# A two-layer AdaLN transformer on one Trainium2 core: 25 first expert blocks instead of 22, finer weight loads, split products, fused norms and products of zeros at the start

## The reference, cut to what matters

```python
# layer 0 (mod = silu(L0_c) @ L0_wmod gives per image: shifts sa, sb, scales ca, cb, gains ga, gb)
h = _layernorm(x) * (1 + ca) + sa
x = x + ga * attention(h)            # 16 query heads, 4 key heads of 128, rms-normed q and k, causal softmax, @ Wo
h = _layernorm(x) * (1 + cb) + sb
x = x + gb * ffn0(h)                 # shared expert + 8 experts of 176, top 2 by sigmoid scores
# layer 1 (mod from L1_c, L1_wmod)
h = _layernorm(x) * (1 + ca) + sa
x = x + ga * linear_attention(h)     # q, k, v of 128; num / den with a memory M, z; @ w_o
h = _layernorm(x) * (1 + cb) + sb
x = x + gb * ffn1(h)
# ffn1(x):
t = xf * rsqrt(mean(xf * xf) + EPS) * norm_w
vals, idx = top_k(t @ gate_w.T + gate_b, 4);  G = softmax(vals) scattered to 16 experts
h = einsum('mh,eoh->emo', t, w1) + b1
a = minimum(h[..., ::2], 7);  b = clip(h[..., 1::2], -7, 7)
y = einsum('emi,edi->emd', a * sigmoid(1.702 * a) * (b + 1), w2) + b2
delta = einsum('me,emd->md', G, y);  return x + delta
```

## Time and profile before

| | us |
|---|---|
| median of 3 runs | 1037.21 (1035.75 to 1038.29) |
| profiled execution, its own time | 1028.9 |
| its span, first to last instruction | 1026.8 |
| PE busy in the span | 961.5 (94%) |
| DVE, ACT, POOL busy | 724.0, 673.0, 425.0 |
| granted TensorE clock, mean | 0.981 |

### The profile page before, as it was taken

How to read it: one execution, slowest core, us unless ns; L and a number is a source line. 1 busy time by engine, 2 the same in 40 slices (tenths; PEclk the granted TensorE clock), 3 DMA queues, 4 the chain that set the end, 5 groups by cost and what they waited for, 6 DMA issues and landing times.

```text
span 1026.8 us, 20504 instructions
## 1 busy us (share of the span) xinstructions
PE 961.5 (94%) x6020; PEld 816.3 (79%) x6020; DVE 724.0 (71%) x2545; ACT 673.0 (66%) x1944; POOL 425.0 (41%) x447
## 2 busy tenths in 40 slices
PE   6999999999999999999999999997889989999970
PEld 4769878888987887887888788886668879999970
DVE  3565656777776777778679677874888868888870
ACT  2656767668668757858776876783745557777740
POOL 2322421332371362156137215414155655566672
PEclk9999999999999999999999999998999999999995
DMA  9926993895699620011012004226357898899944
GB/s 306 305 91 205 377 377 112 307 377 185 235 366 374 230 85 2 4 73 63 1 53 85 1 2 167 74 114 260 84 165 170 227 251 228 214 225 225 225 107 82
DMA packets 93677, 180.53 MB, mean 176 GB/s; under 512 B 9901, under 2 KB 29037, under 8 KB 92669
## 3 DMA queue, kind: packets, MB, share of 16 engines
q1 hardware_dynamic: 73467, 148.55, 43.6%
q0 software_dynamic: 18752, 30.30, 13.1%
q10 hardware_dynamic: 1346, 0.36, 0.2%
HBM read 77.71 MB, written 107.99 MB: 181 GB/s over the span
## 4 chain that ended last, share of the span: by engine, by line
PE 83%; DVE 7%; issue 3%; DMA 2%; ACT 1%; POOL 1%; ACTq 0%; DVEq 0%; SPq 0%; POOLq 0%
PE bank L1101 12%; PE bank L1065 10%; PE bank L1037 10%; PE bank L1110 5%; PE bank L1055 5%; PE bank L1027 5%; PE bank L1016 4%; PE bank L987 3%; PE bank L893 3%; PE bank L1056 3%; PE bank L902 3%; PE bank L1046 2%; PE bank L1026 2%; PE bank L971 2%; PE bank L1009 2%
## 5 line engine op out<-in xcount | busy, mean ns | idle before, releaser
L1896 POOL TENSOR_TENSOR RB<-RB 128x512 f32<-128x512 f32 x64 | 66.7, 1042 | 276.1 <-DVE RB L1675 275.9
L1101 PE MATMUL bank<-RB 128*128 128x128 f32 x1264 | 154.9, 276 | 5.2 <-ACT RB L1373 2.3
L1101 PEld LDWEIGHTS bank<-RB 128*128 128x128 f32 x1264 | 147.9, 192 | 8.0 <-ACT RB L1373 3.2
L1366 ACT ACTIVATE RB<-RA,nw 128x512 f32 x158 | 105.4, 715 | 44.1 <-PE bank L1101 16.5
L1065 PE MATMUL bank<-RA,RB 128*128 128x256 f32 x512 | 132.4, 381 | 0.0
L1037 PE MATMUL bank<-RA 128*128 128x256 f32 x512 | 121.3, 380 | 0.0
L1037 PEld LDWEIGHTS bank<-RA 128*128 128x128 f32 x512 | 94.7, 190 | 14.9 <-issue 3.2
L1065 PEld LDWEIGHTS bank<-RA,RB 128*128 128x128 f32 x512 | 91.3, 190 | 13.0 <-issue 2.3
L1872 POOL TENSOR_TENSOR qs<-qs,half 128x4 f32<-128x4 f32 x64 | 65.6, 1025 | 63.6 <-DVE qs L1684 55.9
L1110 PE MATMUL bank<-RB,BC 128*128 128x256 f32 x316 | 82.0, 383 | 3.7 <-DVE BC L1802 3.6
L1267 ACT ACTIVATE RB<-bank 128x256 f32<-128x256 f32 x128 | 48.7, 381 | 44.0 <-PE bank L1056 43.3
(11 more groups left out here) (251 smaller groups left out, 2389.3 us busy)
## 6 DMA issues: line engine op xcount, KB each, us to landing
xsD<-BC SPq DMA_DIRECT2D x17, 4232.0 KB, 32.8
RB<-in_w2b SPq DMA_DIRECT2D x79, 256.0 KB, 3.7
RB<-xsD SPq DMA_DIRECT2D x61, 264.5 KB, 3.7
BC<-modD SPq DMA_DIRECT2D x16, 512.0 KB, 4.3
X<-xsD SPq DMA_DIRECT2D x18, 264.5 KB, 3.2
RA<-in_w SPq DMA_DIRECT2D x2, 2048.0 KB, 7.3
RA<-in_w SPq DMA_DIRECT2D x6, 512.0 KB, 8.8
RA<-in_L_attn_Wq SPq DMA_DIRECT2D x1, 2048.0 KB, 14.0
```

Source lines behind the costliest of these rows:

```text
L1101: m = pe.matmul(ps[:, 128 * j:128 * j + 128], WS[:, n % 2, c, 128 * j:128 * j + 128], XT[:, n % 2, c * 128:c * 128 + 128], start=(c == 0), ...
L1366: m = act.activation(WS[:, n % 2, c, :], W1[:, bass.ds(r, 1), c, :].rearrange("p a n -> p (a n)"), ACT.Copy, scale=nw[:, c:c + 1])
L1896: pool.tensor_tensor(sq, qrow, qrow, ALU.mult).then_inc(mine("q_sq", p), 1)
```

## The change

It does seven things.

- **25 first blocks** (FIRST 22 to 25), so 54 are left for the rest.
- **The bias of the upper half on ScalarE**: in a first block a new ACT step `e_u` adds the bias (two ACTIVATEs of 128x128 out of PSUM into AB), and `e_b` becomes one DVE `tensor_scalar` of 128x256, SBUF to SBUF, a min with 8. The rest keeps the old `e_b`.
- **Finer weight loads**: W1's last experts come in 8 steps instead of 3, each issued when the operands of attention that lie there are done with; behind `wo(127)` only one expert (9) is left, 512 KB.
- **Split products**: `h_mm` becomes `h_m0` (first 4 products) and `h_mm` (last 4), two steps that the planner can place apart.
- **Three banks**: `h_mm` of first blocks turns through banks 2, 3, 5 instead of 2, 3, and `y_mm` has bank 4 alone instead of 4, 5.
- **Fused norms**: for layer 1, and image 7 of layer 0, `ln_x` no longer waits for POOL's `ln_rs`: it forms (x - mean) * scale in one `scalar_tensor_tensor`, and `f_add` multiplies by the -1/2 power and adds the shift in another; `f_mul` is gone there. `res` takes two operations of 128x512 instead of four of 128x256; `den` one instead of two.
- **Products of zeros**: 10 bf16 products of 128x512 into bank 7 before `modc_mm(0)` and 6 more before `k_mm(0, 0)`.

The planner's weights, landing times and allowances have new values as well, which moves steps everywhere from image 1 on. Some of it:

```diff
-FIRST, PART = 22, 5
+FIRST, PART = 25, 5
-DURING, BEHIND = {5: 0, 6: 0}, {5: -1.1, 6: 0, 7: 0}
+ALLOWED = {"keys": (0.04, -3.638), "query": (0, 1.63), "first": (0.1, 0.187), ...
+DURING, BEHIND = {5: 0, 6: 0}, {5: -0.01, 6: 0, 7: -0}
-HOP, LANDING = 0.2, {"bc": 5.0, "mod_store": 4.0, "clear": 14.0, "w12": 11.0, "xb": 3.2, "w2x": 3.5, ...
+HOP, LANDING = 0.2, {"bc": 5, "mod_store": 4, "clear": 14, "w12": 6, "xb": 3.2, "w2x": 1.9, ...
+W1_PARTS = (
+    ((("pv", NU - 17), ("k_mm", NB - 1, 1), ("v_mm", NB - 1, 0), ("v_mm", NB - 1, 1)), (4, 6), (10, 11), (12, 13)),
+    ((("wo", NU - 13),), (6, 7)),
+    ((("q_mm", NU // 2 - 1),), (0, 4), (14, 15)),
+    ((("wo", NU - 9),), (7, 8)),
+    ((("wo", NU - 5),), (8, 9)),
+    ((("scores", NU - 1),), (11, 12), (15, 16)),
+    ((("pv", NU - 1),), (13, 14)),
+    ((("wo", NU - 1),), (9, 10)),
+)
@@ block(n)
-        yield do("h_mm", n, bank=2 + n % 2, first=True, after=[("w_in", n)] + [("h_mm", n - 1)] * (n > 0))
-        yield do("e_a", n, bank=2 + n % 2, ...
-        p.chain(FILL, clamp(n))
+        yield do("h_m0", n, bank=(2, 3, 5)[n % 3], first=True, after=[("w_in", n)] + [("h_mm", n - 1)] * (n > 0))
+        yield do("h_mm", n, bank=(2, 3, 5)[n % 3], after=[("h_m0", n)])
+        yield do("e_a", n, bank=(2, 3, 5)[n % 3], ...
+        p.chain("block", upper(n))
-        yield do("y_mm", n, bank=4 + n % 2, first=True, ...
+        yield do("y_mm", n, bank=4, first=True, ...
+    def upper(n):
+        yield do("e_u", n, bank=(2, 3, 5)[n % 3], last=True, after=[("e_a", n)] + [("y_mm", n - 3)] * (n >= 3))
+        yield do("e_b", n)
@@ tensor
+            def blanks(n):
+                on.wait_ge(blank_set, 1)
+                for _ in range(n):
+                    pe.matmul(bank[7][:, :], blank[:, 0:128], blank, start=True, stop=True)
+
+            blanks(10)
             def k_mm(b, t):
+                if (b, t) == (0, 0):
+                    blanks(6)
@@ scalar
+            def e_u(n):
+                on.wait_ge(*done("e_a", n))
+                if n >= 3:
+                    on.wait_ge(*done("y_mm", n - 3))
+                for j in range(2):
+                    m = act.activation(AB[:, n % 3, 128 * j:128 * j + 128], psum("e_u", n)[:, 256 + 128 * j:384 + 128 * j], ACT.Identity, bias=b1[:, 2 + j, bass.ds(ex[n], 1)])
+                m.then_inc(mine("e_u", n), 1)
@@ vector: ln_x (whole: layer 1, and image 7 of layer 0), f_add, res, e_b
+                    if whole:
+                        m = dve.scalar_tensor_tensor(dst[:, t, :], X[:, j + t, :], mv[:, j + t, 0:1], BC[:, (b % 3, 4 + b % 2)[k // 2], 512:768], ALU.subtract, ALU.mult)
+                    m = dve.scalar_tensor_tensor(v["hh"][:, t, :], v["xn"][:, t, :], rs[:, j + t, 1:2], BC[:, (b % 3, 4 + b % 2)[l], 256:512], ALU.mult, ALU.add)
-                for t in range(2):
-                    j = 2 * b + t
-                    dve.tensor_tensor(tmp[:, t, :], ps[:, t * 256:t * 256 + 256], g, ALU.mult).then_inc(ch.sem, ch.up())
...
+                dve.tensor_tensor(tmp, pair(ps[:, :]), row(l, b, 0), ALU.mult).then_inc(ch.sem, ch.up())
+                on.wait_ge(ch.sem, ch.n)
+                dve.tensor_tensor(x, x, tmp, ALU.add).then_inc(mine("res", l, b), 1)
+                if n < FIRST:
+                    on.wait_ge(*done("e_u", n))
+                    m = dve.tensor_scalar(AB[:, n % 3, :], AB[:, n % 3, :], 8.0, None, ALU.min)
```

More of the change, by code:

```diff
@@ L39 @@
         "count_on_pe": "n_mm n_pre n_sel", "count_on_dve": "n_blk n_tab n_bi",
-        "block_on_pe": "x_t h_mm y_mm", "block_on_act": "w_in x_out e_tanh", "block_on_dve": "e_a e_b e_g e_act y_out",
+        "block_on_pe": "x_t h_mm y_mm", "half_on_pe": "h_m0", "block_on_act": "w_in x_out e_u e_tanh", "block_on_dve": "e_a e_b e_g e_act y_out",
         "b2_on_pe": "g_t g_mm", "b2_on_dve": "g_add",
@@ L51 @@
     for engine, stages in {
-        "PE": "n_mm .25 n_pre .2 n_sel .95 x_t .25 h_mm 1.8 y_mm .95 g_t .25 g_mm .95 h_t .45 k_mm 1.72 v_mm 1.72 k_t .45 mod_mm 1.72 modc_mm 3.6 f_t .45 f_gate .9 f_rank .4 s_mm 1.2 s_t .22 d_mm .3 d_t .42 d_y 2.15 "
-              "p_t .33 scores .67 q_mm 1.73 q_t .45 pv .65 wo .87 qk_mm 1.73 vv_mm .87 ls_mm .65 num .56 o1_t .22 wo1 .87",
-        "ACT": "w_in 1.45 x_out .38 e_tanh .43 g_out .4 h_mod 1.05 k_sq 1.6 v_out .6 f_ht .62 f_hb .62 f_sig .2 f_sq .9 f_src .9 f_gb .6 f_exp .7 s_tanh .3 s_at .38 d_tanh .35 d_at .7 "
[5 rows of a table removed]
+        "PE": "n_mm 0.25 n_pre 0.2 n_sel 0.95 x_t 0.24 h_m0 0.9 h_mm 0.9 y_mm 0.95 g_t 0.25 g_mm 0.95 h_t 0.45 k_mm 1.72 v_mm 1.72 k_t 0.45 mod_mm 1.72 modc_mm 3.6 f_t 0.44 f_gate 0.9 f_rank 0.43 s_mm 1.2 s_t 0.21 d_mm 0.3 d_t 0.42 d_y 2.15 "
+              "p_t 0.33 scores 0.67 q_mm 1.73 q_t 0.45 pv 0.65 wo 0.87 qk_mm 1.73 vv_mm 0.88 ls_mm 0.65 num 0.56 o1_t 0.22 wo1 0.87",
+        "ACT": "w_in 1.36 x_out 0.38 e_u 0.49 e_tanh 0.43 g_out 0.4 h_mod 1.05 k_sq 1.6 v_out 0.6 f_ht 0.62 f_hb 0.64 f_sig 0.2 f_sq 0.91 f_src 0.9 f_gb 0.6 f_exp 0.7 s_tanh 0.3 s_at 0.38 d_tanh 0.35 d_at 0.7 "
[5 rows of a table added]
     }.items()
@@ L196, in norm, with scaled @@
         yield do("ln_rs", k, b)
+    def scaled(k, b, before, then):
+        yield do("ln_var", k, b)
+        yield do("ln_rs", k, b, aside=True)
+        yield do("ln_x", k, b, after=before)
+        yield do("f_add", k // 2, b, slot=1, after=[("ln_rs", k, b)] + then)
     def to_h(l, b, *after):
@@ L427, in last_weights @@
     def last_weights():
[L428 to L430 removed]
+        for i, (free, *parts) in enumerate(W1_PARTS):
+            yield do("w12", i, by=16 * len(parts), aside=True, after=list(free))
     def block(n):
@@ L446, in block @@
         yield do("e_act", n, after=[("e_b", n)])
-        yield do("y_mm", n, bank=4 + n % 2, first=True, after=[("w2x", n)] + [("y_mm", n - 1)] * (n > 0))
-        yield do("y_out", n, bank=4 + n % 2, last=True, after=[("y_add", n - 5)] * (n >= 5))
+        yield do("y_mm", n, bank=4, first=True, after=[("w2x", n)] + [("y_mm", n - 1)] * (n > 0))
+        yield do("y_out", n, bank=4, last=True, after=[("y_add", n - 5)] * (n >= 5))
         yield do("y_add", n, slot=n % 2, by=16, after=[("tok", n)] + [("y_add", n - 2)] * (n >= 2))
@@ L505, in lay_out @@
             if n > lo:
-                p.add("h_mm", n, bank=bk, first=True)
+                p.add("h_m0", n, bank=bk, first=True)
+                p.add("h_mm", n, bank=bk)
             p.add("e_a", n, bank=bk)
@@ L1470, in ln_x @@
             def ln_x(k, b):
-                j = 2 * b
-                on.wait_ge(*done("ln_rs", k, b))
+                j, whole = 2 * b, k == 3 or (k, b) == (1, NB - 1)
+                on.wait_ge(*(done("ln_var", k, b) if whole else done("ln_rs", k, b)))
                 if k == 0:
```

215 lines of the change are left out of this document (104 added, 111 removed), and 10 rows, old and new, of the table ENGINE.

## The result

The changed kernel took 1043.62 us (median of 11 runs, 1039.62 to 1047.75), the kernel before 1037.21 on the same chip (11 runs, 1035.52 to 1039.42): a ratio of 1.0064, 95% interval 1.0052 to 1.0076. The forecast was 1027.7, faster. The profiled execution of after took 1045.9 us (span 1043.8, mean granted clock 0.971); that of before 1028.9 (span 1026.8, clock 0.981), which is less than any of the 11 runs of before beside the result. So the two traces differ by 17 us where the medians differ by 6.4. What follows shows why: the page of before comes from an execution without a disturbance that the trace of after has, and by their times the 11 runs of before beside the result had it too.

What follows compares the result with a forecast made beforehand. TensorE was taken to set the pace almost everywhere, so gains lie only where it idles or runs at low clock. Start 1.0, end of attention 3.0 and 721.7 to 830 5.5 sum to 9.5: 1037.2 - 9.5 = 1027.7 us, range 1023 to 1032.

Steps and rivals of the forecast that it cites:

- The sum's base: Sum made in the profiled execution of before, 1028.9 us; the same gain taken off the median, 1037.2, 8.3 above.
- Start: Before `q_mm(0)`: products of zeros raise TensorE's clock, gain 1.0 us, range -1.6 to +2.0.
- The two cases of the sum: At the start, clock raised: gain at most 2.0 us, or 0.1 if a wait for Wq lowers the clock again.
- The other edits in attention: Fused norms, `res` and `den` relieve VectorE beside a gapless TensorE: 0; the new order can cost or give 1 us.
- End of attention: 705.4 to 721.7: first expert product near 714.5, 7 us earlier, since one load lands sooner; gain 3.0 us.
- 721.7 to 830: Three more first blocks fill TensorE's idle time during image 7's routing, idle 16 to 10 us; gain 5.5 us.
- rival B: 721.7 to 830: image 7's chain takes the added blocks in full; gain 3.5 us, 1034 us; chance 0.14.
- C: Rival, first blocks: ScalarE's `e_u` holds them up, slower, 1040 us, with all of it 1045; chance 0.10.
- A: Rival: everything is filled, image 7's chain does not stretch and the clock stays up; gain 17, 1020 us; chance 0.22.
- E: Rival: zeros leave the clock low and the first block waits for its load until 717; gain 4, 1033 us; chance 0.07.
- D: Rival, first blocks: `e_b` on VectorE and GpSimd exclude each other, 0.3 us a block; gain 2, 1035 us; chance 0.04.
- my signs for being wrong: Low clock longer than 10 us, TensorE's waits for `e_u` or `e_b` above 5 us, or the rest beginning behind 836.

Runs made afterwards that it cites:

- e1: The kernel before, unchanged, on chip 15, where no trace has late TensorE signals (a quiet chip): 1027.15 us.
- e9: The kernel before, unchanged, traced on chip 11, where TensorE signals come late (a loud chip); last product ends at 1008.0 us.
- e13: The changed kernel, unchanged, on chip 8 (quiet): 1025.06 us, ratio 0.9973 to the kernel before on the same chip.
- e4: The kernel before plus only the 10 + 6 products of zeros, on chip 15 (quiet): 1025.46 us, ratio 0.9985.
- e3: The changed kernel without its products of zeros, on chip 15 (quiet): 1026.36 us, ratio 0.9999 to the kernel before.
- e18: The changed kernel, unchanged, on chip 11 (loud): 1041.08 us, ratio 1.0044 to the kernel before on the same chip.
- e17: The changed kernel with the 16 scatters of images 4 and 5 replaced by 64-byte copies (output wrong), chip 11 (loud): 1034.02 us, ratio 0.9960 to before.
- e7: The changed kernel with `e_b` whole on VectorE and no `e_u`, on chip 0 (loud): 1042.24 us, ratio 1.0058 to the kernel before.
- e5: The changed kernel, unchanged, on chip 0 (loud): 1039.30 us, ratio 1.0037 to the kernel before on the same chip.
- e10: The changed kernel with each scatter of images 4 and 5 waiting until the one before has landed, chip 11 (loud): 1064.84 us, ratio 1.0265 to before.
- e14: The changed kernel with the scatters of images 4 and 5 spaced by the planner, chip 8 (quiet): ratio 1.0107 to the kernel before.
- e15: The kernel before with the scatters of images 4 and 5 spaced by the planner, chip 8 (quiet): ratio 1.0162 to the kernel before.

## Why the prediction was wrong, by its own steps

**The sum's base failed, and with it the sign.** The step was: "I make the sum in the profiled execution and take the gain off both", with the median 8.3 above it. The 8.3 are not a constant. By e1 and e9 they are late signals and low clock on a loud chip, an interaction of the order with the chip, and the change moves exactly the order. The trace of before could not show it, having none. That a profiled execution lay below the lowest of the runs was the sign that I saw and passed over. On quiet chips, for which the sum was in effect made, after is faster, by 2.4 us (e13) instead of 9.5; on loud ones slower by 3.2, 3.3 and 6.4. So two things failed: the base, by 5.6 to 8.8 us, which turned the sign, and the gain itself, by 7.1. From `q_mm(0)` to the last product e13 takes 977.5 us and e1 977.9: behind the start the change brings 0.4 us where 8.5 were forecast.

**Start, +1.0: mis-sized.** 2.0 in the traces of the two kernels, 2.6 between e1 and e13, 1.5 to 2.7 in the times of e4 and e3. The case without a new gap came about in the result's trace: PE waits only 0.62 us for Wq. The two cases of the sum are both real, as the three executions without the gain show (0.6 between e9 and e18).

**The other edits in attention, 0 (within 1): wrong by 2.3 even on a quiet chip.** `q_mm(0)` to the end of `wo(127)` is 686.8 us in e1 and 689.1 in e13, with the same products in it. PE idles 0.6 us more there; where the other 1.7 go stays open. On a loud chip it is 695: this is where the row of image 5 now lies, from 687 on, and where PE soon stands before `pv` without `p_tout`. e17 prices images 4 and 5 at some 6 of it. The new order, which I had costed at nothing, is the largest loss of all.

**End of attention, first product 7 us earlier: right in its mechanism.** From the end of `wo(127)` to the first expert product pass 6.9 us (e13) instead of 14.5 (e1), and it comes at 712.8, where the forecast, less the start's gain, had 712 to 713.5. As said, ACT waits with `w_in(0)` for the last load (after's timeline, where all is later by the late signals; the last two loads are issued from 711.52):

```profile
711.52 1.94 SPq L855 DMA_DIRECT2D RA<-in_w  x2
...
718.71 1.33 ACT L1383 ACTIVATE RB<-RA,nw 128x512 f32 x2 [5.74 <-DMA RA<-in_w]
```

**721.7 to 830, +5.5: rival B came true.** To block 25, past which both kernels run the same rest, the gain from the end of `wo(127)` on is 133.2 - 129.8 = 3.4 us (e1, e13), not 3.0 + 5.5; with start and attention, 3.4 + 2.6 - 2.3 = 3.7. The chain of image 7 took the blocks: `wo1(7)` starts 5.1 us earlier, the count of the blocks ends 5.1 later (timelines, e1 then e13).

```profile
783.44 1.13 PE L1178 MATMUL bank<-RB,SC 128*128 128x256 f32 x4 [1.02 <-ACT SC L1402]
...
809.48 0.29 PE L1084 MATMUL bank<-SC,ecol 16*1 16x80 f32 x2
```
```profile
778.33 1.13 PE L1195 MATMUL bank<-RB,SC 128*128 128x256 f32 x4 [0.70 <-ACT SC L1427]
...
814.57 0.29 PE L1095 MATMUL bank<-SC,ecol 16*1 16x80 f32 x2
```

The windows from the first block to block 25 (e1, e13) show that PE's idle time did not fall either, 17.0 and 17.6 us, where I had it fall from 16 to 10.

```profile
720.70:839.40 118.70, 101.74 (x726) 87.27 (x727) 93.14 (x322) 66.49 (x155) 61.73 (x63) 0.99 0.68 175
```
```profile
712.80:835.70 122.90, 105.29 (x743) 92.54 (x742) 94.94 (x309) 82.57 (x211) 63.25 (x66) 0.97 0.63 162
```

**Rivals.** C, the one with my slower sign, was the wrong mechanism: without `e_u` it is no faster (e7), and PE's waits for it come to 2.1 us in e13. A is out and E too, by the start and the first product. D was given no run, but the traces size it. In e13 22 of the 25 `e_b` of first blocks take 0.28 to 0.33 us and three 0.48 to 0.61, all beside work of POOL: 0.7 us in all and not 0.3 for each. On loud chips D's collision costs more, once: in e5, e17, e18 and the result's trace one `e_b` runs beside POOL's product `f_gain` (L1948) and takes 2.2 to 2.3 us. PE then waits for the `y_out` that stands behind it on DVE (e18):

```profile
832.46 2.25 DVE L1818 TENSOR_SCALAR BC<-BC 128x256 f32<-128x256 f32 x1
...
832.89 1.66 POOL L1948 TENSOR_TENSOR SC<-SC,BC 128x512 f32<-128x512 f32 x1
...
836.65 1.19 PE L1127 MATMUL bank<-RB,BC 128*128 128x256 f32 x2 [2.81 <-DVE X L1843]
```

None of mine was that the order meets something that the trace of before does not hold. (In the chances, the fifth of 0.25 and the 0.02 of C make 0.07 for same, not 0.06; nothing hangs on it.)

**Of my signs for being wrong** two held: the rest's block 25 behind 836 (857.2 in after's trace; 835.7 in e13), and the low clock longer than the 10 us of before. The window 720.10 to 857.20 with its mean of 0.91 has some 24 us of it; in e13 it is again some 10 from `wo(127)` on. Low clock and waits in 832 to 844 of after's trace (window, and ACT's wait) are again late signals, behind the row of image 7:

```profile
836.00:840.00 4.00, 2.50 (x6) 1.63 (x6) 3.26 (x6) 3.12 (x8) 2.80 (x3) 0.50 0.82 176
```
```profile
835.37 1.33 ACT L1383 ACTIVATE RB<-RA,nw 128x512 f32 x2 [5.46 <-remote]
```

**What stays open.** What holds TensorE's signals back physically, why only on some chips, and why a row hurts from its fifth scatter or so on. Whether it is the chip itself or something beside it at that time. The result's trace takes 7.7 us more than e18 from the first block to block 25 and has two "remote" waits there (L1390 and L1383, 3.5 and 5.5) that e18 does not show as such; that late signals are the cause is likely, not shown. No version was found that beats both kernels on both kinds of chip: before with the zeros (e4) is faster than before by 1.5 us on chip 15 and was not run on a loud one.

## What to carry to other kernels

If the profiled execution does not lie among the timed runs, its trace is of another machine state than the number to be predicted: get a trace of that state first. Look in the waits for releases without an instruction, several engines starting at once long after what they wait for; they mark a disturbance that an order can run into or avoid. Back-to-back indirect scatters are cheap on the issuing queue (1.27 us each) and may be dear elsewhere. To lay them where TensorE waits anyway is an idea that no run here tested. To space them with a wait that blocks the queue lost 24 us (e10 beside e18), and to let the planner space them lost 13 and 17 us on a quiet chip (e14, e15).

## What the hardware showed unexpectedly

TensorE's semaphore signals can be held 3 to 4 us and come in one burst, on chips 0 and 11 and in none of the eight traces of 15 and 8, near rows of eight scatters issued 1.27 us apart. The kernel before takes 1027 us on one sort of chip and 1036 to 1038 on the other, its runs on one chip within 0.7% but for one; those of after spread over 1.0% on chip 0. In all three traces of after on loud chips a stretch mostly at half clock follows the late signals near 698 (0.66, 0.57 and 0.62 over 698 to 706; in the result's trace 21 records of PE instead of 46). One VectorE operation of 0.28 us took 2.25 beside a GpSimd product of 1.66.
